# Expert results kept in 64 dense SBUF blocks in place of one result scatter per padded expert block

## The reference

```python
logits = jnp.einsum('btc,ec->bte', x, router_w)
top_vals, top_idx = jax.lax.top_k(logits, 2)
gates = jax.nn.sigmoid(top_vals)
gate, up = jnp.split(jnp.einsum('nc,ech->neh', xf, gate_up_w), 2, axis=-1)
out_all = jnp.einsum('neh,ehc->nec', jax.nn.silu(gate) * up, down_w)
moe = jnp.einsum('ne,nec->nc', w_full, out_all)      # w_full: the two gates, else 0
shared = jnp.einsum('bts,cs->btc', jax.nn.silu(sg) * su, shared_down_w)
return x + moe + shared
```

## Time and profile before

| what | us |
|---|---|
| median of 3 executions | 264.24 (263.43 to 267.71) |
| the profiled execution, its own time | 265.36 |
| its span, from the first to the last instruction | 263.5 |
| PE busy in the span | 226.2 |
| DVE busy | 171.9 |
| ACT busy | 119.2 |
| POOL busy | 139.4 |
| mean granted TensorE clock, share of full | 0.941 |

### The profile page before, as it was taken

One profiled execution on the slowest core, in us unless ns is written; L12 is line 12 of the kernel. 1 busy time (PEld: TensorE's weight loads), 2 busy tenths in 40 slices (PEclk: granted clock), 3 DMA queues, 4 the chain that ended last, 5 costly groups with the idle time before them and its releaser, 6 DMA issues.

```text
span 263.5 us, 5153 instructions
## 1 busy us (share of the span) xinstructions
PE 226.2 (86%) x1306; PEld 174.4 (66%) x1307; DVE 171.9 (65%) x674; ACT 119.2 (45%) x316; POOL 139.4 (53%) x148
## 2 busy tenths in 40 slices
PE   6998998998888986999879899899889889979910
PEld 2555776776776664578758588588678678758810
DVE  3879888988988757352456547547647626732595
ACT  2687657667746120411225536536536625641200
POOL 0000017777777676765006777777777767776000
PEclk9999999999999599569999999999999979998995
DMA  7960001111111111159441333333333333200897
GB/s 229 440 280 2 1 0 52 53 57 54 54 51 51 40 56 40 61 87 142 84 106 44 96 89 104 94 98 106 83 104 90 104 105 86 68 26 0 295 392 269
DMA packets 23797, 27.63 MB, mean 105 GB/s; under 512 B 4654, under 2 KB 19125, under 8 KB 23650
## 3 DMA queue, kind: packets, MB, share of 16 engines
q1 hardware_dynamic: 16370, 15.89, 20.8%
q0 software_dynamic: 4608, 8.47, 9.9%
q10 hardware_dynamic: 2800, 3.04, 4.2%
HBM read 15.70 MB, written 12.73 MB: 108 GB/s over the span
## 4 chain that ended last, share of the span: by engine, by line
PE 58%; DVE 27%; issue 7%; ACT 4%; ACTq 3%; DVEq 0%
PE pKVN L1009 9%; PE pZ L1003 7%; PE pQ L1003 7%; PE pN L820 4%; PE pT L995 4%; PE pKV L830 4%; DVE ZB L517 3%; PE pT L998 3%; PE pZ L806 3%; PE pZ L902 3%; DVE c_stat L477 3%; PE pKVN L820 2%; PE pQ L820 2%; PE pT L806 2%; DVE att L544 2%
## 5 line engine op out<-in xcount | busy, mean ns | idle before, releaser
L325 POOL DMA_INDIRECT results<-Y,XS x80 | 77.8, 972 | 41.5 <-ACT Y L422 23.7
L316 POOL DMA_INDIRECT routed<-ZB,ROWS x64 | 61.4, 960 | 61.4 <-DVE ROWS L613 42.4
L698 DVE COPY xhT<-pT 128x256 f32<-128x256 f32 (+1 forms) x83 | 34.4, 414 | 17.8 <-PE pT L998 16.4
L1009 PEld LDWEIGHTS pKVN<-WF,xhT 128*128 128x128 f32 x160 | 26.9, 192 | 15.3 <-issue 13.4
L1009 PE MATMUL pKVN<-WF,xhT 128*128 x160 | 35.3, 303 | 1.5 <-ACT Y L422 1.5
L422 ACT ACTIVATE Y<-pKVN,XS 128x128 f32<-128x128 f32 x80 | 29.4, 367 | 5.3 <-PE pKVN L1009 2.3
L995 PE MATMUL pT<-CN,XS 128*128 128x128 f32 x80 | 23.0, 288 | 8.3 <-issue 7.0
L1003 PE MATMUL pZ<-WF,xhT 128*128 x80 | 24.7, 391 | 0.0
L709 DVE TENSOR_TENSOR sh_h<-pN,sh_s 128x512 f32<-128x512 f32 x16 | 11.0, 690 | 20.3 <-ACT sh_s L427 10.1
L1003 PE MATMUL pQ<-WF,xhT 128*128 x80 | 24.3, 386 | 0.0
L418 ACT ACTIVATE sg<-pZ 128x128 f32<-128x128 f32 x40 | 11.1, 278 | 27.2 <-PE pZ L1003 27.2
(11 more groups left out here) (129 smaller groups left out, 422.5 us busy)
## 6 DMA issues: line engine op xcount, KB each, us to landing
XS<-routed SPq DMA_DIRECT2D x80, 65.0 KB, 1.8
ZB<-results SPq DMA_DIRECT2D x8, 512.0 KB, 6.8
WF<-w_ffn SPq DMA_DIRECT2D x1, 3456.0 KB, 14.4
X<-x SPq DMA_DIRECT2D x8, 256.0 KB, 5.0
out<-X ACTq DMA_DIRECT2D x8, 256.0 KB, 3.6
results<-Y,XS POOLq DMA_INDIRECT x80, 2.3
routed<-ZB,ROWS POOLq DMA_INDIRECT x64, 2.3
routed<-pad SPq DMA_DIRECT2D x11, 65.0 KB
```

Source lines behind the costliest of these rows:

```text
L316: nc.gpsimd.indirect_dma_start(routed, bass.IndirectOffsetOnAxis(ap=ROWS[:, q, t, k:k + 1], axis=0), Z[:, q, t, k, :], None).then_inc(scat ...
L325: nc.gpsimd.indirect_dma_start(results, bass.IndirectOffsetOnAxis(ap=XS[:, j, D:D + 1].bitcast(U32), axis=0), Y[:, j, :], None, bounds_che ...
L698: nc.vector.tensor_copy(xhT[:, j % 2, a:b, :], pXH[:, a:b, :]).then_inc(s_xhT, 1)
L1009: nc.tensor.matmul(pY, xhT[:, (j + 3) % 2, 1, :], WF[:, 2 * EXP_DIM:][:, bass.ds(w, D)], start=True, stop=True).then_inc(s_D, 1)
```

## The change

- **Items in place of blocks.** The pairs, in order of expert, make up 64 dense blocks of 128 positions. An item is one expert's part of one such block; there are at most 64 + 15 = 79, and the loop still makes 80 steps. Item n is loaded as 128 rows of its expert's region, so placed that each row lies at its position in the dense block; rows that are not the expert's are zeros, so each region now has 128 zero rows ahead of its rows (17 early DMAs from `pad`) and 128 behind them (16 DMAs, all from SP, 128 partitions of one row each in place of 16 partitions of eight).
- **Results gathered in SBUF.** `Y` has 65 blocks of 130 columns, cleared early by two DMAs from `pad`. VectorE adds an item's gated result and its pair numbers into the block, at an address from a register: `gather`, in place of ScalarE's `scaled`. `down` of item n-4 waits for `gather` of item n-5 (`s_acc`). VectorE does a TENSOR_LOAD of 16 block addresses each turn.
- **64 result scatters.** POOL scatters a dense block when all items that reach it are done; it loads the item counts to wait for with 27 single loads behind its last `routed` scatter. No row is skipped. An `XS` slot is free as soon as `gather` has read it.
- **Engines.** The copy `pXH` to `xhT` moves from VectorE to ScalarE (`item_t`), and `pXH` gets a second PSUM tile.
- **Order.** `AHEAD` goes from 7 to 5: four halves are finished ahead of the loop, and 7 lie behind it (`AFTER` = 9). The silu table is loaded ahead of the last copy of `Z`.
- **The tables.** The chain from the counts to the tables has one more matmul (`end`), three matmuls in place of one for the sums, and four in place of two for the rows.

The core of the diff:

```diff
-AHEAD = 7
+AHEAD = 5
 AFTER = AHEAD + TURNS - 1
@@ SP
+            for at in values(sp, pad_at[0:1, :], EXPERTS * REGION):
+                sp.dma_start(routed[bass.ds(at, P), :], pad[:, 0, :]).then_inc(t_pads, 16)
@@ load
-                        wait(sp, ysc[j // 2], it * 32)
-                    sp.dma_start(XS[:, j, :], routed[bass.ds(at[j] * P, P), :]).then_inc(xs[j], 16)
+                    if j % 2 == 0 and not first:
+                        sp.wait_ge(s_acc, it * BODY + (j + 2 - BODY))
+                    sp.dma_start(XS[:, j, :], routed[bass.ds(at[j], P), :]).then_inc(xs[j], 16)
@@ POOL
-            def scatter(it, apart):
-                for j in range(BODY):
-                    if j % apart == 0:
-                        wait_apart(pool, s_y, it * BODY + (j + apart))
-                    nc.gpsimd.indirect_dma_start(
-                        results, bass.IndirectOffsetOnAxis(ap=XS[:, j, D:D + 1].bitcast(U32), axis=0),
-                        Y[:, j, :], None, bounds_check=PAIRS - 1, oob_is_err=False).then_inc(ysc[j // 2], 16)
+            last = [b for b in range(BLOCKS) if b < 4 or b >= BLOCKS - 4 or (not 16 <= b < 52 and b % 2 == 1) or b % 4 == 3]
+            pool.wait_ge(t_table, 2)
+            need = [pool.value_load(done[0:1, b:b + 1], min_val=1, max_val=ITEMS) for b in last]
+            for b in range(BLOCKS):
+                if b == 0 or b - 1 in last:
+                    at = next(i for i in range(len(last)) if last[i] >= b)
+                    wait_apart(pool, s_acc, need[at])
+                nc.gpsimd.indirect_dma_start(
+                    results, bass.IndirectOffsetOnAxis(ap=Y[:, b * YROW + D:b * YROW + D + 1].bitcast(U32), axis=0),
+                    Y[:, b * YROW:b * YROW + D], None).then_inc(ysc[b % 4], 16)
@@ ACT
+            def item_t(n, j, rows=True, hid=True):
+                a, b = (0 if rows else 1), (2 if hid else 1)
+                act.wait_ge(s_T, n + 1)
+                wait(act, s_D, n - 4)
+                if rows:
+                    wait(act, s_gu, n - 1)
+                nc.scalar.copy(xhT[:, j % 2, a:b, :], pXH[j % 2][:, a:b, :]).then_inc(s_xhT, 1)
-            def scaled(n, j):
-                act.wait_ge(s_D, n + 1)
-                nc.scalar.activation(Y[:, j, :], pY, ACT.Copy, scale=XS[:, j, D + 1:D + 2]).then_inc(s_y, 1)
+                    item_t(n, j, hid=not (first and j < 3))
                     if not (first and j < 1):
                         silu(n - 1, (j - 1) % BODY)
-                    if not (first and j < 4):
-                        scaled(n - 4, (j - 4) % BODY)
@@ DVE
+            def gather(n, j, y):
+                wait(dve, s_acc, n)
+                index = Y[:, D:].bitcast(U32)[:, bass.ds(y, 1)]
+                nc.vector.tensor_tensor(index, XS[:, j, D:D + 1], index, ALU.add)
+                dve.wait_ge(s_D, n + 1)
+                part = Y[:, bass.ds(y, D)]
+                nc.vector.scalar_tensor_tensor(part, pY, XS[:, j, D + 1:D + 2], part,
+                                               ALU.mult, ALU.add).then_inc(s_acc, 1)
                     if not (first and j < 2):
                         hidden(n - 2, (j - 2) % BODY)
-                    transposed(n, j, hid=not (first and j < 3))
+                    if not (first and j < LEAD):
+                        gather(n - LEAD, (j - LEAD) % BODY, y[j])
@@ PE
             def down(n, j, w):
-                wait(pe, s_y, n)
+                pe.wait_ge(s_xhT, n + 4)
+                wait(pe, s_acc, n)
```

More of the change, by code:

```diff
@@ L248, in has, with values @@
             return 0 <= s - lag < NQ
-        def values(eng, row, start, count, most):
+        def values(eng, row, most):
             return nc.values_load_multi_w_load_instructions(
-                row[0:1, bass.ds(start, count)], engines=(eng.engine,), min_val=0, max_val=most,
+                row, engines=(eng.engine,), min_val=0, max_val=most,
                 skip_runtime_bounds_check_because="the table is clamped where it is made")[1]
-        def pads(eng, first, count):
-            for at in values(eng, pad_at, first, count, EXPERTS * REGION - P):
-                eng.dma_start(routed[bass.ds(at, P), :].rearrange("(p r) c -> p r c", p=PAD_PARTS),
-                              pad[:, :, :]).then_inc(t_pads, 16)
         block = ctx.enter_context(nc.Block())
@@ L271, in _ @@
             sp.dma_start(WF[:, :], w_ffn).then_inc(s_wf, 16)
[L274 to L283 removed]
+            sp.wait_ge(t_pad, 1)
@@ new lines, in _ @@
+            for g in range(EXPERTS + 1):
+                sp.dma_start(routed[g * REGION:g * REGION + P, :].rearrange("(p r) c -> p r c", r=PAD_ROWS),
+                             pad[0:P // PAD_ROWS, :, :]).then_inc(t_still, 16)
+            sp.dma_start(Y[:, 0:BLOCKS * YROW].rearrange("p (a f) -> p a f", f=PAD_ROWS * ROW),
+                         pad[:, :, :].rearrange("p r c -> p (r c)").unsqueeze(1)
+                         .to_broadcast([P, BLOCKS // PAD_ROWS, PAD_ROWS * ROW])).then_inc(t_zero, 16)
@@ new lines, in _, with rows, load @@
+            sp.dma_start(Y[:, BLOCKS * YROW:], pad[:, 0, :]).then_inc(t_zero, 16)
+            sp.wait_ge(t_still, 16 * (EXPERTS + 1))
+            sp.wait_ge(t_pad, 2)
+            for at in values(sp, pad_at[0:1, :], EXPERTS * REGION):
+                sp.dma_start(routed[bass.ds(at, P), :], pad[:, 0, :]).then_inc(t_pads, 16)
+            def rows(it):
+                return values(sp, table[0:1, T_ROW, bass.ds(it * BODY + LEAD, BODY)], EXPERTS * REGION)
+            def load(it, at, first):
@@ L427, in shared @@
                 nc.scalar.activation(sh_s[:, :], pSG[pair][:, :], ACT.Silu).then_inc(h_silu, 1)
-            shared(0)
-            act.wait_ge(t_pad, 2)
-            for i in range(1, AHEAD):
-                if i <= ACT_PADS // 2:
-                    pads(act, EXPERTS - ACT_PADS + 2 * (i - 1), 2)
+            for i in range(AHEAD):
                 shared(i, i % 2)
@@ L448, in _ @@
                 body(it, False)
-            silu(BLOCKS - 1, BODY - 1)
-            for k in range(4, 0, -1):
-                scaled(BLOCKS - k, BODY - k)
+            for k in range(3):
+                item_t(ITEMS + k, k, rows=False)
+                if k == 0:
+                    silu(ITEMS - 1, BODY - 1)
             for i in range(AFTER, HALVES):
@@ L768, in _ @@
                 body(it, False)
-            for k in range(3):
+            y = values(dve, table[0:1, T_Y, ITEMS:ITEMS + LEAD], BLOCKS * YROW)
+            for k in range(LEAD):
                 if k < 2:
-                    hidden(BLOCKS - 2 + k, BODY - 2 + k)
-                transposed(BLOCKS + k, k, rows=False)
+                    hidden(ITEMS - 2 + k, BODY - 2 + k)
+                gather(ITEMS - LEAD + k, BODY - LEAD + k, y[k])
             def total(q):
@@ L1042, in _ @@
             pe.wait_ge(t_tab, 1)
-            for a in range(2):
-                i = nc.tensor.matmul(pZ[0:1, 128 + a * P:128 + (a + 1) * P], table_f[:, a:a + 1], ident, start=True, stop=True)
-            i.then_inc(t_row, 1)
+            for a in (T_ROW, T_EXP, T_Y):
+                nc.tensor.matmul(pZ[0:1, (a + 1) * P:(a + 2) * P], table_f[:, a:a + 1], ident, start=True, stop=True)
+            nc.tensor.matmul(pZ[0:1, 64:64 + BLOCKS], ones[:, 0:1], within[:, :], start=True, stop=True).then_inc(t_row, 1)
             for i in range(1, AHEAD - 1):
```

193 lines of the change are left out of this document (103 added, 90 removed).

## The result

| | before | after |
|---|---|---|
| median of 4 executions each | 265.98 (263.43 to 273.36) | 301.75 (300.25 to 306.55) |
| ratio, 95% interval | 1 | 1.142 (1.135 to 1.148) |
| span of the profiled execution | 263.5 | 298.4 |
| mean granted TensorE clock | 0.941 | 0.910 |

The ratio and its interval compare only executions within 1.5% of the fastest of their kernel (two of the four of before), so the ratio is above 301.75 / 265.98 = 1.134.

What follows compares the result with a forecast made beforehand. The prediction took PE's plain step, set by `pY`, as the bound, not POOL. Span 263.5 - 5.9 (start) + 6.8 (loop) + 1.8 (behind it) = 266.2, then + 1.86 - 1.12 = 266.9 us; range 258 to 274.

Steps and rivals of the forecast that it cites:

- The register loads: At a turn's end in the loop: VectorE's load of 16 numbers, about 1.1 us, hidden under PE's own of 1.5.
- busy-DMA case: Dearer loads: SyncE's before the loop at 3.2 instead of 1.1 us; POOL's 27 at 3.2 each, end near 310, chance 0.03.
- The clock: TensorE's clock in the loop: nothing added, though PE idles 0.25 of each plain step in place of 0.15.
- third rival: Loop steps grow by more, up to 1.29 us, through address work and extra waits: 278, halfway 273; chance 0.22.
- The plain step: Loop step without a shared half, `down` to `down`: 1.12 us, 50 x 0.10 = 5.0 us more in all.
- second circle: Loop over two steps: PE's order, silu, h, index sum, `gather`, `down`; 2.245 us, 1.12 a step, 1.34 with a shared part.
- `pY`'s circle: In each plain step, `down`, `gather`, next `down` through one PSUM tile: 0.49 + 0.04 + 0.335 + 0.13, put at 1.00 us.
- hand-overs: Gaps in the plain step: 0.04 us from `down`'s end to `gather`, 0.13 from `gather`'s end to the next `down`.
- this sign: In plain steps, `gather` starts when the index sum lets it; if it waits for `down`, the forecast is wrong.
- The loop's start: Ahead of the loop: start at 127.4, 5.9 us earlier than 133.32, between 126.8 and 131; first `XS` load at 125.0.
- POOL and its single loads: Beside PE's steps: 16 scatters fewer given nothing; 27 loads at 0.34 to 0.7 us, POOL up to 8 us late, level again.
- Behind the loop: After the last `down`: seven halves, set by VectorE at 3.6 us for each of three; 15.1 in place of 13.3, +1.8 us.

## Why the prediction was wrong, point by point

**The register loads (wrong, the largest error).** The step "VectorE's register load at a turn lies under PE's own of 1.5", and with it the unchanged pause, took the price of a load from the earlier trace rows by its count alone. The rows of after were 3.1 times as dear, and the diff held the reason: `LEAD` went from 4 to 5 and the rows of the table became 133 words. I had priced a dearer load only for SyncE and POOL, as a busy-DMA case. Aligned, the time falls by 15.1 us. A number cost 0.21 to 0.29 us in the unaligned loads and 0.07 in the aligned ones of 20 (1.49 us).

**The clock (wrong, and it follows from the loads).** The forecast adds nothing for the clock: it takes the loop to lose it at one turn in four, as before. Only the third rival, at 273, had it lost at more turns, and how often was an estimate. It was lost at every turn (+6.0 us), with pauses that had risen from 1.8 to 4.9 us; the kernel before with PE's table one word off shows the same, with nothing else changed. Over all profiles, behind pauses below 1.7 us the clock was full (1.00) in all but one (0.67 behind 1.48 us, in the kernel that only multiplies), behind those of 4.6 and more it was half (0.50 to 0.63), and between 1.7 and 2.3 us both occur (1.00 behind 1.81, 1.89 and 2.27; 0.58, 0.61 and 0.57 behind 1.77, 1.80 and 2.11). No sharp limit follows from these rows.

**The plain step (wrong in size and in mechanism).** The forecast was 1.12, by a second circle through h; the step was 1.22 to 1.27, by `pY`'s circle, which I had put at 1.00. `gather`'s own 0.335 was near the measured 0.35. What failed were the hand-overs, 0.04 and 0.13, taken over from the rows of before: they are 0.15 and 0.24. The diff held both reasons. `gather` has a computed address, so a register instruction stands between `down` and it (0.10), and `down` has a second wait, so one more instruction stands between `gather` and it (0.11); VectorE's 0.35 is 0.02 shorter than ScalarE's 0.37. Together 1.02 + 0.10 + 0.11 - 0.02 = 1.21, and 1.22 was measured. The third rival, "the step grows by more" (up to 1.29), named address work and extra waits on VectorE and PE, the two things that it was, but in a chain through h, and put the end at 278. I had said the forecast would be wrong if `gather` waited for `down`; with the order exchanged it did, and the step was the same, so this sign could not tell the two circles apart.

**The second circle (right only for other steps, and too short there).** For a step with a shared part it gave 1.34; they were 1.40 to 1.51, and fell to 1.31 when `gather` went ahead of h.

**The loop's start (wrong).** Forecast -5.9 us, measured -1.7. The first `XS` load came at 129.46 instead of 125.0. Of these 4.5 us, 2.2 were there already at SyncE's load of `pad_at` (115.1 against 112.9), which is within the spread between executions. Most of the rest is the last `routed` scatter, which landed 4.2 us behind its start (in the chain) where I had 2.3. That 2.3 was a misreading: before's trace holds no landing for the last eight scatters, so the 2.3 of the earlier trace rows comes from earlier ones, and the kernel before with two `pY` has 4.9 for its last. Before's own rows showed it: its first `XS` load stands at 127.79, 5.5 us behind the start of the last scatter at 122.3. And PE's own load ran from 127.0 to 131.7, so that PE would not have started earlier even with data. The pads themselves were right: 8.63 us against 8.8.

**POOL and its single loads (right).** 16 scatters less gave nothing in this loop. POOL's 27 single loads took 0.28 us each (the middle value; the first took 0.66) and started from 122.7 to 137.3. The first scatter was at 138.7 and the last at 270.0, 0.7 us behind the last `down`'s matmul.

**Behind the loop (right).** Forecast +1.8, measured +1.7. VectorE's products stand 3.6 us apart, as forecast:

```profile
286.72 0.68 DVE L724 TENSOR_TENSOR eq<-pN,rq 128x512 f32<-128x512 f32 x1
...
290.30 0.68 DVE L724 TENSOR_TENSOR eq<-pN,rq 128x512 f32<-128x512 f32 x1
```

**The account.** From 301.75 down: alignment 15.1 us, `gather` ahead of h 5.0, 20 numbers 1.3, the computed address 7.2; and, measured on the kernel before, the exchange of engines with its second wait 4.5 (by the interval, anything from 0 to 6). That is 33.1 of the 35.8 us between the medians (37 between the executions that the ratio uses). Several of these differences are no larger than the spread of one kernel's executions, and they were taken in three sets, so that the sum comes so close is in part luck; the remainder of 2.7 says little. 1.7 us lie behind the loop by the trace.

## What to carry to other kernels

When a change moves a table that registers are loaded from, work out the byte at which each load starts, counted from the start of the tensor: here a load of 20 numbers took 1.47 us from a multiple of 16, and 5.0 from one word further on. Load whole fours, even if some numbers are not used, where the trace shows it pays: here 20 took 1.49 us and 19 took 1.90. When an instruction that TensorE waits for changes its form or its engine, add up the circle again with everything that stands between a semaphore and the instruction behind it: here a computed address cost 0.10 us of every step, and a second wait on TensorE, for something already waited for, 0.11. A second bank for the PSUM tile was worth more than any of these (21 us; the change then beats the kernel before by 2.5%, 0.975 with an interval of 0.964 to 0.986, and by about 2% the kernel before with a second bank of its own, 264.31). Work saved on an engine beside the bound, as POOL's 16 scatters here, showed up only once the bound itself had been moved: with two `pY` the last of 64 scatters started at 234.0, the last of 80 at 241.2.

## What was not expected of the hardware

- A register load of 20 numbers took 1.47 us from a multiple of 16 bytes behind its tensor's start and 5.0 us one word further on. 19 aligned numbers took 1.90 us, 20 took 1.49.
- From the end of a VectorE or a ScalarE instruction to the TensorE instruction that waits for its semaphore it was 0.04 us, the same for both. With a computed weight address the matmul stood 0.13 behind that end, and with a second semaphore wait 0.24.
- On VectorE, a multiply by a scalar for each partition (128x128, PSUM to SBUF) took 0.35 us, and multiply and add with a third operand 0.35 as well.
- Behind pauses of 1.7 to 2.3 us TensorE came back at full clock (1.00 over 4 us) or at half (0.57 to 0.72), with no sharp limit, and once at half (0.67) behind a pause of 1.48. Four steps that took 5.2 us behind a pause at full clock, in the kernel before and in those with `gather` ahead of h, took 6.1 to 6.9 at half.
